# Cross-attention and feed-forward kernel: another first PSUM bank for the projections, and the gathering copies one step earlier on ScalarE

## What is computed

```python
x = x + xattn(_layernorm(x), ctx_2048, ...)
x = x + ffn(_layernorm(x), ...)

# xattn
q = rms_norm(linear(x, q_w, q_b), norm_q_w)
k = rms_norm(linear(ctx_txt, k_w, k_b), norm_k_w);  v = linear(ctx_txt, v_w, v_b)
k_img = rms_norm(linear(ctx_img, k_img_w, k_img_b), norm_k_img_w);  v_img = linear(ctx_img, v_img_w, v_img_b)
out = attention(q, k, v) + attention(q, k_img, v_img)
return linear(out, o_w, o_b)

# ffn
x_norm = layer_norm(x, in_gamma, in_beta)
thought = x_norm[:, -1, :] @ agg_w + agg_b
for _ in range(4):
    t = layer_norm(thought, pn_gamma, pn_beta)
    t = gelu(t @ d1_w + d1_b)
    thought = thought + (t @ d2_w + d2_b)
broadcast = (thought @ bc_w + bc_b)[:, None, :]
gate = sigmoid(x @ gate_w + gate_b)
return layer_norm(x + gate * broadcast, out_gamma, out_beta)
```

## Time and profile before

| | us |
|---|---|
| median of 3 runs | 519.63 |
| lowest, highest | 519.60, 520.52 |
| the profiled execution | 518.58 |
| its span, first to last instruction | 516.8 |

### The profile page before, as it was taken

One profiled execution on the slowest core, in us unless ns is written; L12 is line 12 of the kernel. 1 busy time (PEld: TensorE's weight loads), 2 busy tenths in 40 slices (PEclk: granted clock), 3 DMA queues, 4 the chain that ended last, 5 costly groups with the idle time before them and its releaser, 6 DMA issues.

```text
span 516.8 us, 9804 instructions
## 1 busy us (share of the span) xinstructions
PE 494.6 (96%) x3734; PEld 319.4 (62%) x3734; DVE 351.0 (68%) x781; ACT 302.7 (59%) x548; POOL 254.5 (49%) x157
## 2 busy tenths in 40 slices
PE   8999999999899999999999999999999999999990
PEld 7988878777666666656665555454544455545440
DVE  5379846877787778749784876565656485427677
ACT  4883466543276667736873466666663566667553
POOL 1330033320067779848886544352525374739563
PEclk9999999999999999999999999999999999999996
DMA  8997577497997799986999793525252473000011
GB/s 286 390 301 268 198 163 230 166 213 278 275 261 186 189 309 205 250 229 181 238 275 235 182 267 112 127 68 132 64 137 64 139 202 123 6 22 22 26 37 61
DMA packets 61439, 91.92 MB, mean 178 GB/s; under 512 B 4496, under 2 KB 29344, under 8 KB 60816
## 3 DMA queue, kind: packets, MB, share of 16 engines
q1 hardware_dynamic: 56992, 74.68, 53.9%
q0 software_dynamic: 3280, 14.51, 8.8%
q10 hardware_dynamic: 1120, 2.10, 1.3%
HBM read 71.87 MB, written 19.66 MB: 177 GB/s over the span
## 4 chain that ended last, share of the span: by engine, by line
PE 78%; DVE 13%; ACT 3%; DMA 3%; issue 2%; DVEq 0%; SPq 0%; ACTq 0%
PE psum L876 13%; PE psum L984 13%; PE psum L1003 13%; PE psum L967 12%; PE psum L1051 6%; PE psum L1008 5%; PE psum L1160 3%; PE psum L1096 3%; PE psum L1116 3%; DMA qscr<-hl 2%; PE psum L898 2%; DVE hl L1481 1%; DVE negt L1494 1%; DVE hl L1480 1%; PE psum L881 1%
## 5 line engine op out<-in xcount | busy, mean ns | idle before, releaser
L1266 ACT ACTIVATE prob<-psum 128x512 f32<-128x512 f32 x256 | 138.9, 595 | 97.1 <-PE psum L984 78.3
L1494 DVE TENSOR_REDUCE negt<-psum 128x1 f32<-128x512 f32 (+1 forms) x256 | 133.1, 546 | 17.3 <-PE psum L967 17.1
L1770 POOL TENSOR_TENSOR added<-added,prob 128x1024 f32<-128x1024 f32 x48 | 114.7, 2389 | 11.8 <-ACT prob L1266 7.0
L984 PEld LDWEIGHTS psum<-qst,kst 112*128 112x128 f32 x512 | 77.2, 188 | 36.0 <-ACT prob L1266 17.1
L984 PE MATMUL psum<-qst,kst 112*128 112x256 f32 x512 | 97.8, 307 | 1.3 <-ACT prob L1266 1.0
L1767 POOL TENSOR_TENSOR added<-prob 128x1024 f32<-128x1024 f32 x16 | 38.0, 2374 | 112.9 <-ACT prob L1266 112.9
L967 PE MATMUL psum<-kst,qst 96*128 96x512 f32 x256 | 85.3, 429 | 4.8 <-DVE negt L1494 3.6
L1003 PE MATMUL psum<-prob,vring 128*32 128x256 f32 x1152 | 83.5, 387 | 0.3 <-ACT prob L1266 0.3
L1492 DVE TENSOR_REDUCE negt<-psum 128x1 f32<-128x257 f32 x128 | 53.0, 414 | 45.2 <-PE psum L967 45.1
L967 PEld LDWEIGHTS psum<-kst,qst 96*128 96x128 f32 x256 | 42.8, 188 | 35.1 <-issue 15.7
L1003 PEld LDWEIGHTS psum<-prob,vring 128*32 128x32 f32 x1152 | 27.6, 108 | 20.9 <-ACT prob L1266 0.8
(11 more groups left out here) (189 smaller groups left out, 711.7 us busy)
## 6 DMA issues: line engine op xcount, KB each, us to landing
kst<-kscr SPq DMA_DIRECT2D x96, 256.0 KB, 6.3
vring<-vscr SPq DMA_DIRECT2D x16, 576.0 KB, 7.2
kscr<-hl SPq DMA_DIRECT2D x16, 512.0 KB, 3.2
d<-d POOLq DMA_DIRECT2D x8, 1024.0 KB, 9.3
qst<-qscr SPq DMA_DIRECT2D x48, 128.0 KB, 4.2
vscr<-vbuf SPq DMA_DIRECT2D x18, 256.0 KB, 3.3
qscr<-hl SPq DMA_DIRECT2D x8, 512.0 KB, 3.0
in_c<-ctxT SPq DMA_DIRECT2D x2, 1024.0 KB, 13.1
```

Of the source, the lines that this page charges most:

```text
L984: mm = pe.matmul(score2[:, j * QH:(j + 1) * QH], kst[0:96 + 4 * HPG, slot, jj, k0:k0 + P], qst[0:96 + 4 * HPG, slot, jj, :], start=True, s ...
L1266: act.activation(prob[:, r % NP, part], score2[:, part], ACT.Exp).then_inc(exp2_done, 1)
L1494: dve.tensor_reduce(negt[:, u % 2, qt, half, HPG + j:HPG + j + 1], psum[:, tile_bank[n], k0:512], AX.X, ALU.max, negate=True)\
L1770: pool.tensor_tensor(added[:, :], added[:, :], prob[:, r % NP, :], ALU.add).then_inc(added_done, 1)
```

## The change

Two edits. The jobs ahead of `S1(0)` take the banks in the same turn, but from another first bank: `first_bank` = (6 + 1 - 50) % 8 = 5, so that job 49 lies in bank 6 (`SUM_BANK`). And `ch_gather` is put at the end of step 73, right behind `ch_agg`, in place of within step 74.

```diff
@@ make_plan
         if k == 0:
             behind(s + 1, 'ch_agg', 0)
-            at(s + 2, 'ch_gather')
+            behind(s + 1, 'ch_gather')
             at(s + 2, 'ch_stat', 2)
@@ build
     n_s1 = sum(in_plan[e] < in_plan[('S1', 0)] for e in jobs)
-    bank_of = [n % 8 if n < n_s1 else SHARED_BANK if n > last_v or e[0] == 'shift' else 3 + (n - n_s1) % 4 for n, e in enumerate(jobs)]
+    first_bank = (SUM_BANK + 1 - n_s1) % 8
+    bank_of = [(n + first_bank) % 8 if n < n_s1 else SHARED_BANK if n > last_v or e[0] == 'shift' else 3 + (n - n_s1) % 4 for n, e in enumerate(jobs)]
```

## The result

The changed kernel takes 517.45 us (median of 20 runs), where the kernel before takes 519.62 (20 runs); the ratio is 0.9956, with a 95% interval of 0.994 to 0.9972, so 1.5 to 3.1 us less. The forecast was 518.2. The profiled execution takes 516.72 us with a span of 514.9, against 518.58 and 516.8 before. The sign and the place are as forecast, and the size is within the range, but the experiments show that the difference of the medians is made of more than the stall that was counted.

A forecast was written before the change was run, and what follows sets the result against it. TensorE bounds the kernel, busy 494.6 of 516.8 us, so gains must come from its stalls or waits within groups. Edit 1 at 0 and edit 2 at −1.4 us take 519.63 to 518.2 us, range 517.0 to 519.7.

The forecast's parts named there:

- Edit 1 at 0: First score tiles, `S1(0)`: tile 1's stall goes, but VectorE's queue still holds tile 3 to 104.16 us; worth 0.
- The bound of −1.21 us: In front of score tile 1 of `S1(0)`: the most edit 1 could gain, the whole stall of 1.21 us.
- Edit 2 at −1.4 us: Step 75: copies made earlier bring statistics, maxima and exponentials forward, so `PV(75)` starts at 309.5 to 309.7; gain 1.4 us.
- The floor of 1.21 us: Step 75, start of the `S1` pair to the next `PV`: at best 1.21 us, as one step earlier, against 2.77.
- upper bound of 1.56 us: Step 75: edit 2 gains at most 2.77 − 1.21 = 1.56 us.
- the pessimistic end of the copies: Step 75: copies start only at 306.12, end at 306.84 and delay step 74's exponentials by 0.72 us; gain still 1.0 us.
- It stays: Behind step 75: nothing swallows edit 2's gain; `tT` comes about 1.5 us earlier, `ch_d1` near 312.5 instead of 313.97.
- The rival "slower": In front of tile 3: joined idle time of 1.58 us drops TensorE's clock to 1.2 GHz; 521.1 us, chance 0.07.
- the prediction's own sign of being wrong: Around 104 us: a granted clock under 1.00 would show the forecast wrong.
- The price: Product of 2.93 us behind tile 3: at the lower clock it would take as much again, 2.9 us more.
- place A: `S1(0)`: tile 1 starts at 100.29 us after 1.21 us of idle time that ScalarE's squares end.

The follow-up runs named there:

- the maxima first: Changed kernel with `norm(3,3)` put behind the first `S1` step: 517.71 us, ratio 0.9956; the same with the old banks: 516.98 us, 0.9939.
- the gathering alone: Kernel before with only the gathering copies moved ahead of the exponentials of step 74, banks unchanged: 517.42 and 517.14 us, ratios 0.9931 and 0.9948.
- the bank edit alone: Kernel before with only the banks changed, gathering copies left behind the exponentials of step 74: 521.46 us, ratio 1.0015.

## Why the prediction was right, and where not

**Edit 1 at 0: right in the trace, and for the reason given.** Tile 1 follows tile 0, tile 3 stays where VectorE's maxima put it. That a later tile 3 is a matter of the queue is shown by putting `norm(3,3)` behind. The idle time in front of tile 3 came out at 1.91 us, not 1.58: `proj(5,1,0)` starts 100.63 − 98.99 = 1.64 us earlier, more than the 1.21 us of idle time, since the two tiles now run as one group (0.63 us for both, where they took 0.39 and 0.50). The bound of −1.21 us was too small by that; with the maxima first the place gave 1.57.

**Edit 2 at −1.4 us: the mechanism right, the term too small.** It measured 1.63 us. The floor of 1.21 us was taken from the step before, whose own `S2` took 0.72 us where the one of step 75 now takes 0.64; the free stretch is 1.14 us. My upper bound of 1.56 us was therefore too low. The copies began right behind `ch_agg` and cost the exponentials nothing; I had allowed 0 to 0.3 us. For the pessimistic end of the copies the prediction left a gain of 1.0 us; the copies made twice leave 1.63 − 0.75 = 0.88.

**It stays: right.** `ch_d1` is 312.16 − 314.00 = −1.84 us; 0.18 of it was there before step 75 (`ch_agg` ended at 305.13 in place of 305.31), and the undisturbed spans are 1.2 to 1.6 us shorter.

**The clock: the step that failed.** The rival "slower" had the right mechanism, and I gave it too little. I gave 0.07 to "the joined idle time lets the clock fall", because a gap of 1.4 us at 131 us had left it at 1.00 and 1.58 us seemed hardly longer. In 20 of 43 executions of the changed kernel it fell, by their mean clock, so the prediction's own sign of being wrong, a granted clock under 1.00 around 104 us, came up in about half of them. One profiled execution at 1.00 had said nothing about the others. The price was also off: 1.6 us and not 2.9. The whole product at the lower clock would have cost 2.7 by my estimate (from its start to the next group's start it takes 107.11 − 104.38 = 2.73 us in the changed kernel's profile), but the clock was back before it ended.

I also did not see that the kernel before already paid for its stall at step 75 with a fallen clock, in up to 46 of 88 executions and with 3 us between the median spans. So, as an estimate, edit 2 removes 1.6 us in each and 3 us in about half, some 1.6 + 3.0 × 46/88 = 3.2 us on average, and edit 1 brings back 1.6 × 20/43 = 0.7 us. Together that is 2.4 us, and the ratio says 2.3. The mean spans of these executions, 518.1 before, 515.2 with the gathering alone and 516.0 with both, give 2.9, 0.8 and 2.1. The forecast had 1.4; that its median came as close as it did is partly luck, since these two effects, each unseen, partly cancel.

## What to carry to other kernels

A stall is read at the wait that ends last: removing the wait in front of it only moves the idle time, and joining two short idle times of TensorE can cost more than either, so an edit "worth nothing" on the path isn't free. A row that shows the full clock in one execution does not show it for the others; the mean clock of every run does. A step that heads a chain over three engines belongs ahead of work whose turn has not come, as long as the idle time there is at least as long as the step: the second set of copies cost its full length.

## What the runs showed of the hardware

Behind the 1.9 us in which TensorE stood still in front of tile 3, the granted clock fell to 1.2 GHz for most of the next product in three of the six profiles that have this idle time, and by the mean clocks in about half of the executions; the Trainium skill, "TensorE: Matmul & The Clock Gate", HAM oscillation, says that idle gaps between matmuls bring the throttle back, and by that rule the trace agrees. The waits for DMA in the case told there are longer than this one; here 1.9 us was enough in a part of the executions.

But the length of a gap alone doesn't tell it. In the three profiles of the kernel before, the clock stayed up behind the 1.21 us at tile 1 and the 1.40 us at 131 us. Behind the 0.81 us at step 75 it stayed up in two of them and fell in the third, and it fell there in the profile of the bank edit alone. TensorE's work around that stall is another than at place A, where products of twelve 128x512 matmuls stand on both sides: a run of small matmuls (`ch_agg`, 32 of them in 1.08 us) ended 3.5 us before it, and right behind it a group of four waited within itself (0.99 us in place of 0.64). Whether either of these matters was not tried.

The price of one fall is not fixed either: 1.5 to 1.6 us at place A, and at step 75 2.8 us in one profile (`ch_d1` took 5.04 us there in place of 3.64) and 1.2 us in another, where the clock was back sooner (3.85 us).
